# A two-layer recurrent block on eight cores: attention scores and activations split into half groups, and first projections moved behind the quantization

## What is computed

```python
# layer 0
xn = _layernorm(x)
x_proj = silu(xn @ W1 + b1)               # u, v, q, k; 16 heads of 64
scores = einsum('bqhd,bkhd->bhqk', qh, kh)
attn = silu(scores) / S                   # no softmax
av = einsum('bhqk,bkhd->bqhd', attn, vh)
s = _layernorm(av * u, gamma, beta) @ W2 + b2
g = silu(light_ffn(xn) + heavy_ffn(routed tokens of xn))  # top 1024 of 2048
x = x + s * g
# layer 1
xn = _layernorm(x)
q, k, v = (xn @ fake_quant_int8(W).T + b for each of Wq, Wk, Wv)
probs = softmax(einsum('bhqd,bhkd->bhqk', q, k) / 8)
s = einsum('bhqk,bhkd->bhqd', probs, v)
h = silu(xn @ w1 * s1) * (xn @ w2 * s2)   # 4096 wide
h = gelu(h @ h1 * sh1); h = gelu(h @ h2 * sh2)
x = x + s * silu(h @ w3 * s3)
```

## Time and profile before

| | us |
|---|---|
| median of 2 runs | 7026.91 |
| lowest and highest run | 7023.07, 7030.76 |
| profiled execution | 7024.82 |
| its span on the slowest core (core 3) | 7023.3 |
| spans of the eight cores | 6988.8 to 7023.3 |

### The profile page before, as it was taken

One profiled execution on the slowest core, in us unless ns is written; L12 is line 12 of the kernel. 1 busy time (PEld: TensorE's weight loads), 2 busy tenths in 40 slices (PEclk: granted clock), 3 DMA queues, 4 the chain that ended last, 5 costly groups with the idle time before them and its releaser, 6 DMA issues.

```text
span 7023.3 us, 61050 instructions; the slowest of 8 cores (6988.8 to 7023.3 us)
## 1 busy us (share of the span) xinstructions
PE 5302.2 (75%) x24088; PEld 2087.4 (30%) x24088; DVE 1186.7 (17%) x1753; ACT 1709.7 (24%) x1897; POOL 360.7 (5%) x679
## 2 busy tenths in 40 slices
PE   6666655665666776256666666699999999999999
PEld 3222222111222222022222222144444444444444
DVE  4200111003302212632222222210010001001000
ACT  0244433452101111034444444410011011001101
POOL 0000000000010000000000000010020011002000
PEclk7655555556889998568778878799999999999999
DMA  3000000000363333400000000198899889889988
GB/s 109 6 6 7 7 6 7 0 1 12 78 138 105 107 105 115 141 27 0 1 1 1 1 1 1 33 159 151 153 160 160 151 158 165 151 153 162 159 151 143
DMA packets 153481, 560.01 MB, mean 80 GB/s; under 512 B 16754, under 2 KB 21106, under 8 KB 112244
## 3 DMA queue, kind: packets, MB, share of 16 engines
q0 software_dynamic: 99920, 417.38, 35.0%
q1 hardware_dynamic: 53284, 138.72, 6.2%
HBM read 927.24 MB, written 33.55 MB: 137 GB/s over the span
## 4 chain that ended last, share of the span: by engine, by line
PE 64%; ACT 15%; DMA 8%; DVE 7%; issue 5%; DVEq 1%; ACTq 0%; SPq 0%; POOL 0%; POOLq 0%
PE pb L1458 13%; PE pb L1476 13%; ACT pt L606 7%; PE psA L582 4%; PE pb L1494 3%; ACT pt L1353 3%; PE psA L1431 3%; PE psA L1436 3%; ACT pt L1356 3%; PE psA L547 3%; PE psA L1328 2%; PE psA L873 2%; DVE sqrot L1378 2%; PE psA L1148 2%; DMA w1hb<-w1hS 1%
## 5 line engine op out<-in xcount | busy, mean ns | idle before, releaser
L1458 PE MATMUL pb<-hA,wHb 128*128 128x512 bf16 x4096 | 886.4, 379 | 7.9 <-DVE hA L1445 7.9
L1476 PE MATMUL pb<-hB,wHb 128*128 128x512 bf16 x4096 | 884.7, 379 | 4.5 <-ACT hB L1464 4.5
L606 ACT ACTIVATE pt<-psA 128x2048 bf16<-128x2048 f32 x256 | 480.8, 1878 | 455.2 <-PE psA L582 455.2
L1458 PEld LDWEIGHTS pb<-hA,wHb 128*128 128x128 bf16 x4096 | 400.9, 98 | 493.4 <-issue 12.0
L1476 PEld LDWEIGHTS pb<-hB,wHb 128*128 128x128 bf16 x4096 | 400.5, 98 | 488.7 <-issue 6.3
L582 PE MATMUL psA<-q_p,k_p 64*128 64x512 bf16 x1024 | 260.0, 599 | 306.2 <-ACT pt L606 299.0
L1328 PE MATMUL psA<-q_p,k_p 64*128 64x512 bf16 x1024 | 194.2, 459 | 289.4 <-ACT pt L1356 285.0
L873 PE MATMUL psA<-xng,w1hb 128*128 128x512 bf16 x1024 | 264.8, 411 | 137.9 <-DMA w1hb<-w1ht 51.6
L1507 DVE TENSOR_TENSOR sg<-gt,smix 128x512 f32<-128x512 bf16 x32 | 22.2, 692 | 1964.3 <-ACT gt L1501 1952.9
L1353 ACT ACTIVATE pt<-psA,col_tmpa 128x1024 bf16<-128x1024 f32 x256 | 285.4, 1115 | 221.1 <-PE psA L1328 220.3
L1378 DVE RECIPROCAL sqrot<-sqrot 1x1024 f32<-1x1024 f32 x32 | 209.3, 6541 | 690.0 <-ACT sqrot L1376 690.0
(11 more groups left out here) (318 smaller groups left out, 5187.8 us busy)
## 6 DMA issues: line engine op xcount, KB each, us to landing
wHb<-h1wt POOLq DMA_DIRECT2D x128, 1024.0 KB, 9.2
wHb<-h2wt POOLq DMA_DIRECT2D x128, 1024.0 KB, 9.1
w12b<-w1wt POOLq DMA_DIRECT2D x128, 256.0 KB, 5.3
w12b<-w2wt POOLq DMA_DIRECT2D x128, 256.0 KB, 6.6
wHb<-w3wt POOLq DMA_DIRECT2D x32, 1024.0 KB, 10.6
w1hb<-w1hS SPq DMA_DIRECT2D x96, 256.0 KB, 2.6
w2hb<-w2hS SPq DMA_DIRECT2D x48, 512.0 KB, 3.3
xrot<-xT SPq DMA_DIRECT2D x16, 1024.0 KB, 6.6
```

Source lines behind the costliest of these rows:

```text
L606: sc_ev["s"] = SI(lambda s, ptsl=ptsl: s.activation(pt[:, ptsl, :], psALL[:, :, :], AF.Silu))
L1458: emitter(lambda t, it=it, slh=slh, bank=bank: t.matmul(psB[bank][:, :], wslH[slh][:, it, :], hA[:, it, :], start=(it == 0), stop=(it == 31)))
L1476: emitter(lambda t, it=it, slh=slh, bank=bank: t.matmul(psB[bank][:, :], wslH[slh][:, it, :], hB[:, it, :], start=(it == 0), stop=(it == 31)))
```

## The change

1. Layer 0 attention: the wait for the whole activation is replaced by one before each key tile's two score matmuls. The first pair (banks 0 and 1) waits for half A of the group before, the second pair (banks 2 and 3) for half B. Both pairs now raise PE's semaphore. The activation is split into two of 128 x 1024, half A gated by the first pair, half B by the second.
2. Layer 1 attention: the same gates, by head. The two Exp activations stay as they were; the first one now also raises ACT's semaphore and waits for head 0's scores alone.
3. The first pair's q and k projections are no longer written beside the quantization; every pair projects q and k at the top of the loop, 64 matmuls through banks 0 and 1 in turn with eight DVE evacuations. The working buffers of layer 1 attention are allocated after the quantization, `iq_t` being released first.

```diff
@@ layer 0 attention
                 for grp in range(8):
                     ptsl = grp % 2
-                    wt("t", cs, sc_ev.get("s", 0))
+                    t_half = {}
                     for tkk in range(2):
                         tk = 2 * grp + tkk
+                        wt("t", cs, sc_ev.get("A" if tkk == 0 else "B", 0))
                         for h in range(2):
                             bank = 2 * tkk + h
-                            last = (tkk == 1 and h == 1)
-                            emitter = TI if last else TN
+                            emitter = TI if h == 1 else TN
                             emitter(lambda t, ...: t.matmul(psB[bank][:, :], ...))
+                        t_half[tkk] = ct.n
                     t_sc = ct.n
 ...
+                    wt("s", ct, t_half[0])
+                    wt("s", ct, av_mm.get(ptsl, 0))
+                    sc_ev["A"] = SI(lambda s, ptsl=ptsl: s.activation(
+                        pt[:, ptsl, 0:1024], psALL[:, 0:2, :], AF.Silu))
                     wt("s", ct, t_sc)
-                    wt("s", ct, av_mm.get(ptsl, 0))
-                    sc_ev["s"] = SI(lambda s, ptsl=ptsl: s.activation(
-                        pt[:, ptsl, :], psALL[:, :, :], AF.Silu))
+                    sc_ev["B"] = SI(lambda s, ptsl=ptsl: s.activation(
+                        pt[:, ptsl, 1024:2048], psALL[:, 2:4, :], AF.Silu))
                 ptsl = 7 % 2
-                wt("t", cs, sc_ev["s"])
+                wt("t", cs, sc_ev["B"])
@@ quantization
                 emit_io_chunk(wp, c)
                 emit_reduce(wn, wi, c)
-                if wi == 2 and c % 2 == 1:
-                    tq_last = emit_proj_mms(0, "q", c // 2, c // 2, ...)
-            if wi == 2:
-                for g in range(NTG):
-                    emit_proj_evac(0, "q", g, g, tq_last if g == 0 else None)
             sbc[wn] = emit_dance(wn)
         for c in range(NCH):
             emit_io_chunk("v", c)
-            if c % 2 == 1:
-                tk_last = emit_proj_mms(0, "k", c // 2, c // 2, ...)
-        for g in range(NTG):
-            emit_proj_evac(0, "k", g, g, tk_last if g == 0 else None)
+        sfree("iq_t")
+        q_p2 = sbt("q_p2", [128, T], BF16)   # and k_p2, v_p2, pt2, qsq2, recipb_s
         wt("t", cv, cv.n)
@@ layer 1, top of the loop over pairs
-            if p > 0:
-                for w in ("q", "k"):
-                    for g in range(NTG):
-                        emit_proj_qk(p, w, g)
+            for w, dst, bnm in (("q", None, "bq"), ("k", None, "bk")):
+                for g in range(NTG):
+                    bank = g % 2
+                    wt("t", cv, aev.get(bank, 0))
+                    (eight matmuls, then wt("v", ct, tmm) and the DVE evacuation)
@@ layer 1 attention
-                    wt("t", cs, sc2_ev.get("s", 0))
+                    t_half = {}
                     for h in range(2):
+                        wt("t", cs, sc2_ev.get("A" if h == 0 else "B", 0))
                         for tkk in range(2):
                             bank = 2 * h + tkk
-                            emitter = TI if last else TN
+                            emitter = TI if tkk == 1 else TN
                             emitter(lambda t, ...: t.matmul(psB[bank][:, :], ...))
+                        t_half[h] = ct.n
                     t_sc = ct.n
 ...
-                    wt("s", ct, t_sc)
+                    wt("s", ct, t_half[0])
                     wt("s", ct, pt2_mm.get(ptsl, 0))
-                    SN(lambda s, ptsl=ptsl: s.activation(
+                    sc2_ev["A"] = SI(lambda s, ptsl=ptsl: s.activation(
                         pt2[:, ptsl, 0:1024], psALL[:, 0:2, :], AF.Exp, ...))
-                    sc2_ev["s"] = SI(lambda s, ptsl=ptsl: s.activation(
+                    wt("s", ct, t_sc)
+                    sc2_ev["B"] = SI(lambda s, ptsl=ptsl: s.activation(
                         pt2[:, ptsl, 1024:2048], psALL[:, 2:4, :], AF.Exp, ...))
-                wt("t", cs, sc2_ev["s"])
+                wt("t", cs, sc2_ev["B"])
```

More of the change, by code:

```diff
@@ L1129, in emit_io_chunk @@
             VD()
[L1131 to L1158, removed]
-            aev[bank] = VI(lambda v, w=w, dst=dst, g=g, p=p, bank=bank, bnm=bnm:
-                           v.tensor_scalar(dst[:, g * 512:(g + 1) * 512],
-                                           psB[bank][:, :], scC[w][:, p:p + 1],
-                                           vcs(bnm, p), OP.mult, OP.add))
-        def emit_proj_qk(p, w, g):
-            bank = g % 2
-            tmm = emit_proj_mms(p, w, g, bank)
-            emit_proj_evac(p, w, g, bank, tmm)
         issue_am("q", 0, 0)
@@ L1173, in build_program @@
         sbc["q"] = emit_dance("q")
-        tq_last = 0
         for wi in (1, 2):
@@ L1179, in build_program @@
                 emit_reduce(wn, wi, c)
-                if wi == 2 and c % 2 == 1:
-                    tq_last = emit_proj_mms(
-                        0, "q", c // 2, c // 2,
-                        first_gate=quant_v[("q", "io", NCH - 1)] if c == 1 else 0)
-            if wi == 2:
-                for g in range(NTG):
-                    emit_proj_evac(0, "q", g, g, tq_last if g == 0 else None)
             sbc[wn] = emit_dance(wn)
-        tk_last = 0
         for c in range(NCH):
             emit_io_chunk("v", c)
-            if c % 2 == 1:
-                tk_last = emit_proj_mms(
-                    0, "k", c // 2, c // 2,
-                    first_gate=quant_v[("k", "io", NCH - 1)] if c == 1 else 0)
-        for g in range(NTG):
-            emit_proj_evac(0, "k", g, g, tk_last if g == 0 else None)
+        sfree("iq_t")
+        q_p2 = sbt("q_p2", [128, T], BF16)
+        k_p2 = sbt("k_p2", [128, T], BF16)
+        v_p2 = sbt("v_p2", [128, NTT, 128], BF16)
+        pt2 = sbt("pt2", [128, 3, 2048], BF16)
+        qsq2 = sbt("qsq2", [128, T], BF16)
+        recipb_s = sbt("recipb_s", [128, 512], F32)
         wt("t", cv, cv.n)
+        aev = {}
+        sc2_ev = {}
+        pt2_mm = {}
+        pend = [None]
         def emit_ctx(pgrp, psl, par):
@@ L1244, in build_program @@
                 wt("t", cs, cs.n)
-            if p > 0:
-                for w in ("q", "k"):
-                    for g in range(NTG):
-                        emit_proj_qk(p, w, g)
+            for w, dst, bnm in (("q", None, "bq"), ("k", None, "bk")):
+                dst = q_p2 if w == "q" else k_p2
+                for g in range(NTG):
+                    bank = g % 2
+                    wt("t", cv, aev.get(bank, 0))
+                    for c in range(NCH):
+                        emitter = TN if c < NCH - 1 else TI
+                        emitter(lambda t, w=w, c=c, g=g, p=p, bank=bank: t.matmul(
+                            psB[bank][:, :], wqi[w][:, c, p * 128:(p + 1) * 128],
+                            xn[:, c, g * 512:(g + 1) * 512],
+                            start=(c == 0), stop=(c == NCH - 1)))
+                    tmm = ct.n
+                    wt("v", ct, tmm)
+                    aev[bank] = VI(lambda v, w=w, dst=dst, g=g, p=p, bank=bank, bnm=bnm:
+                                   v.tensor_scalar(dst[:, g * 512:(g + 1) * 512],
+                                                   psB[bank][:, :], scC[w][:, p:p + 1],
+                                                   vcs(bnm, p), OP.mult, OP.add))
             for tt in range(NTT):
@@ L1325, in build_program @@
                             bank = 2 * h + tkk
-                            last = (h == 1 and tkk == 1)
-                            emitter = TI if last else TN
+                            emitter = TI if tkk == 1 else TN
                             emitter(lambda t, tk=tk, g=g, h=h, bank=bank: t.matmul(
```

2 lines of the change are left out of this document (1 added, 1 removed).

## The result

| | before | after |
|---|---|---|
| median of the runs | 7122.08 (10 runs) | 6911.51 (11 runs) |
| lowest and highest | 7022.61, 7398.21 | 6650.88, 7158.16 |
| profiled execution | 7024.82 | 6650.88 |
| its span on the slowest core | 7023.3 (core 3) | 6649.3 (core 5) |

In about half of the executions of either kernel the cores of one die, sometimes of both, have a lower granted clock and the run takes some per cent more; compared without these, the ratio of after to before is 0.9506 [0.9436, 0.9576], so the change makes the kernel about 5% faster. The prediction was 6641 us: the profiled execution lies 10 us above it, and the median of all runs 270 above it, outside the stated range.

A forecast was written before the change was run, and what follows sets the result against it. PE and ACT wait for each other in both attentions because four score banks act as one buffer. Span 7023.3 - 286 - 103 + 3 = 6637 us, plus 1.5 and 2.1, gives 6641 us; range 6585 to 6730.

The forecast's parts named there:

- The mechanism: Both attentions: refilling each pair of banks once its half is read overlaps PE and ACT; 286 and 103 us gained.
- The step from the span to the median: Whole kernel: profiled execution 1.5 us above its span, median 2.1 above that, taking 6637 to 6641 us.
- The group of layer 0: Layer 0 attention: a group falls from 3.21 to 1.97 us, between 1.85 and 2.14; 8.7 us a block from seven gaps.
- The end of the blocks: Layer 0 block ends: 0.41 us gained by the earlier first activation, 0.07 lost at the last half; routing steps unchanged.
- The clock inside the blocks: Layer 0 attention: granted clock rises from 0.50 some us into each block, is low again after routing; above 0.59 overall.
- The first rival: Layer 0: the clock never rises, 2.14 us a group, 250 us gained, 6677 us in all; chance 0.20.
- The second: ACT bounds layer 0 throughout and one head's tiles pair in layer 1; 308 and 113 us gained, about 6606; chance 0.17.
- The group of layer 1: Layer 1 attention, last five groups of a block: 3.03 to 2.35 us each; whole layer gains 103 us, bounds 75 and 125.
- they pair: Layer 1 scores: if one head's two tiles run together, two groups take 4.54 us (2.27 each), otherwise 4.86 (2.43).
- Groups 0 to 2: Layer 1 block heads: still wait for the 6.54 us reciprocal and the broadcasts; no gain or loss counted.
- Group 3's earlier half: Layer 1 attention: group 3's first half comes earlier, giving 0.2 us a block.
- Part 3: Quantization to layer 1's first scores: moving the first projections behind the quantization loses 3 us, bounds -3 and +12.

The follow-up runs named there:

- e1: The kernel before with only layer 0 attention in halves; that stage went from 1319.2 to 1011 us, profiled execution 6772.57 us.
- e2: The kernel before with only layer 1 attention in halves; that stage went from 1467.3 to 1396.1 us, profiled execution 7056.65 us.
- e9: The kernel before plus two unread matmuls per layer 0 group except a block's first; layer 0 attention went from 1319.2 to 1223.6 us.
- e6: The kernel after, each layer 0 half being both key tiles of one head; layer 0 attention 1148.8 us, profiled execution 6781.96 us.
- e4: The kernel after, each layer 1 half being one key tile of both heads, with one bias; layer 1 attention 1395.2 to 1361.8 us, run 6612.05 us.
- e8: The kernel after with layer 1's sums broadcast before the reciprocal and the division written one group earlier; layer 1 attention 1395.2 to 1221.0 us, run 6472.95 us.
- e3: The kernel before with only the first pair's projections moved behind the quantization; that stretch went from 198.4 to 201.2 us, profiled execution 7012.0 us.
- e7: Both attentions in halves, layer 1's by key tile, division off the path, first projections beside the quantization; ratio to the kernel before 0.9183.

## Why the prediction was right or wrong

**The mechanism** was right: the halves overlap, ACT's work stays, its idle time goes, in both layers, and e1 and e2 show it for each part alone. The faster kernel is the predicted one, at 5% and within 10 us of its own profiled execution. That closeness is partly luck: the terms of the two layers were off by 24 and 32 us with opposite signs.

**The step from the span to the median** is the one that failed. "the profiled execution is 1.5 above its span and the median of the runs 2.1 above that" priced it at 3.6 us, from two runs of the kernel before that lay 8 us apart. It measured 262 us: the span of the kernel after is 6649.3, where the sum has 6637, and the median of its eleven runs is 6911.51. The kernel before shows the same, 99 us from its span to the median of ten runs (7023.3 and 7122.08). Its ten runs spread over 376 us and the eleven of the kernel after over 507, for the reason given beside the table of the result, and the range of 6585 to 6730 had no part for that. The one profiled execution could not show it; the spread of two runs was taken for the spread of the kernel.

**The group of layer 0** was right. Predicted 1.85 at the high level, 2.14 at the low one, 1.97 as a mixture; measured 1.81, 2.19 and a mean of 13.66 / 7 = 1.95. Seven gaps fell from 22.43 to 13.66 us, 281 us over 32 blocks (predicted 275: 8.7 a block, less 3 for the pairs' first gaps). The waits in front of the activations cost nothing, as assumed. The ends of the bounds were worked out wrongly: by the prediction's own terms 2.14 a group gives 247 us and 1.85 gives 312, not 250 and 308.

**The end of the blocks** was undersized, and it is 18 of the 24 us (the gaps are the other 6). The prediction gave each block 0.41 - 0.07 beyond its gaps, some 11 us; measured 29. It had priced the last values, the next block's first scores, and the projections behind a pair at the low clock they had before. With the clock up, the 9.7 us from the last activation to the next block's first are 8.97, and the short one of 4.21 is 3.25; one pair boundary went from 38.8 to 36.0. The prediction let the clock act inside the loop and forgot what stands next to it. e9 bears this out: without any halves, its higher clock alone takes 25 us out of the stretches between the blocks.

**The clock inside the blocks.** The prediction weighed here a page against a row. The Trainium skill, "TensorE: Matmul & The Clock Gate" ("HAM oscillation"), gives as its rule that PE should have no idle gap beyond a stated length, which is longer than any rest of PE in layer 0 attention. The row has the clock at 0.50. The prediction's "never rests over 1.2 us inside a block" is nearly so (six rests of 1.5 to 1.6 in 32 blocks), and between the blocks the longest is 2.2, in the kernel before and after alike. The rows decide: e9 raised the clock of that same loop to 0.84 by added matmuls alone, with every wait left in place, and e6 has it at 0.65 with less rest than the kernel after. The first rival (the clock never rises) fell: 0.80 over the stage. The second came nearest for layer 0 (308 of gain against 309.7), though not by its own reason, since the low level does occur and 29 us came from beside the gaps.

**The group of layer 1**'s gain was oversized, and it is 23 of the 32 us. The middle of two bounds, 2.35, was taken; measured 2.53, above the upper bound 2.43. The prediction's loop, 2.12 + 0.15 + 0.43 + 1.39 + 0.77 = 4.86, reads in the timeline as 2.13 (3033.40 to the end of L1333 at 3035.53) + 0.14 + 0.52 + 0.95 + 0.56 + 0.75 = 5.05. Two things were missing. One head's tiles go one after the other, so the bound "they pair" was never open: 0.215 between two starts. And each turn of the array from one shape of matmul to another costs about 0.1 (0.52 for two scores of 0.215 each, and the same behind the values). The prediction had this turn in its pairing case, 0.33 = 0.22 + 0.11, and left it out of the other, where 0.43 is the two scores alone; with it the upper bound is 4.97, or 2.49 a group. That the 0.1 is the change of shape is read from these starts and was not tested by itself. Four gaps a block gave 64 us, not 87. e4 takes the first of the two away and gets 4.65 at the end of a block.

**Groups 0 to 2** were right: 11.91 us from the block's first activation to the one behind the broadcasts, as before. The prediction said that it would be a gain if the reciprocal were gone. e8, which takes it off the path and also writes the division one group earlier, shows how large, 174 us, 2.4 times what the halves brought in this layer. Group 3's earlier half didn't come (4.18 for 4.12), and together with the first blocks of the pairs the head of the block gave 8 us, not 16: the rest of the 32.

**Part 3** was right: +3.0 for +3 on the slowest cores (+4.2 between the medians of eight), and +2.8 in e3 alone.

**Left open.** The stretch between the two attentions is 5 to 10 us longer in the kernel after, while e1, e2, e3 and e9 have it at 1237 to 1241 and e4, e6, e7 and e8 at 1247 to 1248; it isn't touched, and cores differ by as much in one run. Why e6's clock stays low is open.

## What to carry to other kernels

When two engines take turns over one buffer, splitting the buffer can pay twice: by the overlap itself, and by the granted clock. The second is not certain (it rose from 0.59 to 0.80 here, and in e6 only to 0.65); where it comes, price it also for the instructions beside the loop. Before halving, look at which matmuls end up in a half: here two that use different rows of the array ran together (0.39 us), and two that use the same rows did not (0.60). And read the distance from a block's first activation to its steady rhythm before improving the rhythm, because there the larger gain lay (11.9 us, of which the reciprocal on one partition is 6.5).
